# Overlapped Ghost blocks with a reloaded transposed x, look-up masks from ScalarE, and MLP weights through three raw buffers

## The reference

```
xn = layernorm(x)
h = rmsnorm(xn) -> q, k (8 heads x 32), v (8 x 64), output gate o, gates i and f (8 each)
Dmat[s,t] = F[s] - F[t] + i[t], causal;  m = rowmax(Dmat);  C = (q k^T / sqrt(32)) * exp(Dmat - m)
attn = C / max(|rowsum C|, exp(-m)) @ v;  rms norm per head, * sigmoid(o);  x1 = xn + attn @ w_out
attention block = x1 + (silu(rms(x1) @ w_gate) * (rms(x1) @ w_up)) @ w_down          # 512 -> 2048 -> 512
w = lut[idx]  (16 values; gate, up: 1376 x 512, down: 512 x 1376)
Ghost = (silu(xn @ w_g^T) * (xn @ w_u^T)) @ w_d^T                                     # 512 -> 1376 -> 512
```

## Time and profile before

| | before |
|---|---|
| median of three runs | 2892.45 us (2889.81 to 2893.76) |
| the profiled execution: its own time / its span | 2881.09 / 2879.3 us |
| TensorE busy (matmul) | 2558.6 us, 89% |
| VectorE busy | 1382.3 us, 48% |
| ScalarE busy | 837.6 us, 29% |
| GpSimd busy | 628.6 us, 22% |
| mean granted TensorE clock | 0.949 |
| moved | 508.94 MB, 177 GB/s |

### The profile page before, as it was taken

One profiled execution on the slowest core, in us unless ns is written; L12 is line 12 of the kernel. 1 busy time (PEld: TensorE's weight loads), 2 busy tenths in 40 slices (PEclk: granted clock), 3 DMA queues, 4 the chain that ended last, 5 costly groups with the idle time before them and its releaser, 6 DMA issues.

```text
span 2879.3 us, 33321 instructions
## 1 busy us (share of the span) xinstructions
PE 2558.6 (89%) x11152; PEld 2045.8 (71%) x11152; DVE 1382.3 (48%) x2444; ACT 837.6 (29%) x1522; POOL 628.6 (22%) x496
## 2 busy tenths in 40 slices
PE   6667999899899999889989988999889889889888
PEld 5345787687677777768767766777767767767767
DVE  4543645674675675567367466611323313323323
ACT  4323214434433442443443344211111111111111
POOL 2533221221221222132122122211111111111111
PEclk9578999999999999999999999999999999999999
DMA  4555442354255346136435424654654664664664
GB/s 147 209 201 215 147 168 92 132 192 158 96 182 218 103 154 241 63 124 217 155 120 187 177 106 154 234 201 167 249 212 160 245 223 165 245 221 165 248 217 164
DMA packets 121659, 508.94 MB, mean 177 GB/s; under 512 B 11376, under 2 KB 11376, under 8 KB 88080
## 3 DMA queue, kind: packets, MB, share of 16 engines
q1 hardware_dynamic: 115152, 494.89, 48.4%
q10 hardware_dynamic: 6336, 11.80, 1.2%
HBM read 434.69 MB, written 71.96 MB: 176 GB/s over the span
## 4 chain that ended last, share of the span: by engine, by line
PE 44%; issue 38%; POOL 7%; DVE 6%; DMA 2%; ACT 2%; DVEq 0%; POOLq 0%; SPq 0%; ACTq 0%
PE acc L561 10%; PE up_bank L561 9%; PE gate_bank L561 8%; PE bank_b L561 5%; PE bank_a L561 5%; POOL hidden_lo L1648 4%; PE bank_a L637 2%; PE bank_b L634 1%; PE bank_a L596 1%; DMA gu<-mlp_parts 1%; DVE look_w L1244 1%; PE bank_b L644 1%; PE bank_b L626 1%; DMA raw_dn<-w_dn 1%; POOL vw L1679 1%
## 5 line engine op out<-in xcount | busy, mean ns | idle before, releaser
L561 PE MATMUL gate_bank<-act_hi,gu 128*128 128x512 f32 x1728 | 605.4, 412 | 99.5 <-DMA gu<-ghost_parts 71.7
L1648 POOL TENSOR_TENSOR hidden_lo<-hm,hidden_hi 128x512 fp32r<-128x512 f32 x216 | 285.0, 1319 | 1480.2 <-ACT hidden_hi L860 1480.2
L561 PE MATMUL up_bank<-act_hi,gu 128*128 128x512 f32 x1728 | 593.9, 405 | 0.0
L561 PE MATMUL acc<-dn,hidden_hi 128*128 128x512 f32 x1728 | 559.7, 406 | 32.5 <-POOL hidden_lo L1648 32.5
L561 PEld LDWEIGHTS gate_bank<-act_hi,gu 128*128 128x128 f32 x1728 | 341.1, 197 | 184.5 <-issue 105.5
L1249 DVE SCALAR_TENSOR_TENSOR th<-th,gate_bank 128x512 f32<-128x512 f32 x216 | 147.6, 683 | 579.5 <-ACT th L855 579.5
L561 PEld LDWEIGHTS acc<-dn,hidden_hi 128*128 128x128 f32 x1728 | 326.6, 195 | 100.6 <-POOL hidden_lo L1648 20.3
L561 PEld LDWEIGHTS up_bank<-act_hi,gu 128*128 128x128 f32 x1728 | 326.7, 189 | 80.9 <-issue 13.5
L561 PE MATMUL gate_bank<-act_lo,gu 128*128 128x512 f32 x864 | 350.8, 406 | 0.0
L561 PE MATMUL acc<-dn,hidden_lo 128*128 128x512 f32 x864 | 344.2, 398 | 0.0
L561 PE MATMUL up_bank<-act_lo,gu 128*128 128x512 f32 x864 | 338.6, 392 | 0.0
(11 more groups left out here) (213 smaller groups left out, 3204.0 us busy)
## 6 DMA issues: line engine op xcount, KB each, us to landing
gu<-mlp_parts SPq DMA_DIRECT2D x128, 1024.0 KB, 5.2
gu<-ghost_parts SPq DMA_DIRECT2D x89, 1024.0 KB, 5.1
dn<-mlp_parts SPq DMA_DIRECT2D x128, 512.0 KB, 4.8
dn<-ghost_parts SPq DMA_DIRECT2D x88, 512.0 KB, 3.9
ghost_parts<-look_w SPq DMA_DIRECT2D x33, 512.0 KB, 3.0
mlp_parts<-gu SPq DMA_DIRECT2D x16, 1024.0 KB, 4.9
xn<-x SPq DMA_DIRECT2D x15, 1024.0 KB, 7.8
vo_w_hi<-vo_parts SPq DMA_DIRECT2D x12, 1024.0 KB, 9.7
```

Of the source, the lines that this page charges most:

```text
L561: mm = pe.matmul(dst, l[a], r[c], start=first and k == 0 and n == 0, stop=last and k == len(lhs) - 1 and n == 2)
L1648: pool.tensor_tensor(HH[1][:], hm[:], HH[0][:].bitcast(f32), ALU.subtract).then_inc(of.low.sem, 1)
```

## The change

**Ghost part.** Eight blocks written out one behind the other. The last `down` of a block (and that of the last MLP tile) comes behind the next block's `gate(0)` and `up(0)`. In the stage of every block SP stores its transposed x, high and low, to a new DRAM array (2 MB a block), and reloads it in tiles 1 and 2 of the Ghost block before; no layer norm and no transposes there. SP's row transfers stand one a tile in tiles 1 to 6. The sums are added by VectorE behind tile 0's `product` of the next block. The last block's output goes out in four pieces.

**Look-up.** ScalarE makes the masks of bits 1 to 3 as floats that are zero or not, from the index itself (Abs and Relu with constants), so a chunk has seven steps on VectorE beside bit 0 and 14 on ScalarE. Ten chunks for a pair of blocks (five and five), five more in `tiles(TAIL)`. A function `plan` writes out the steps of each tile under the caps ROOM_V and ROOM_A. In a unit's tile VectorE's steps and `norm_1` stand ahead of its `unit_3`. `upper` and `lower` of a chunk are called for in the same tile, SP stores it a tile later. One buffer holds the finished pair.

**MLP weights and the first block.** A tile's three parts are loaded, split and stored together (1536 columns). Tiles 0 to 11 go through two buffers that lie where the second block's transposed x comes later, 12 to 15 through a third. Four are split in `front(FIRST)`, eight beside the units, four in `front(SECOND)`. The second x is loaded into `raw_gu` in tile 1, its statistics taken in tiles 4 and 6. The first block's h2 steps move into `front(SECOND)`, with the ACC banks for the output projection. V and O weights are stored in tile 2 of the second block.

```diff
+PER_PAIR = 10
+CHUNKS = [(0, 5), (5, 10)]
+LEFT = 5
+STEPS_V = 7
+SELECTS = [(2, 3, 1), (5, 4, 1), (1, 0, 1), (6, 7, 1), (2, 1, 2), (5, 6, 2), (2, 5, 3)]
+STEPS_A = ["y", 3, "z", 2, "m1", 4, 5, "m3", 0, 1, 7, "m2", 6, "upper"]
+COUNTED = len(STEPS_A) - 1
+FREED_BY = {3: 4, "m1": 4, 4: 2, 0: 3, 1: 5, 7: 4, "m2": 6, 6: 6, "upper": 7}
+FREED_BY_OTHER = {5: 7, "m3": 7}
+NEEDED = ["m1", 5, 1, 6, 6, 6, 6]
+ROOM_V = [[0, 0] + [2] * 6 + [3, 3] + [4] * 5 + [0]] * 2 + [[3] * 15 + [0]]
+ROOM_A = [[5] * 8 + [7] * 7 + [0]] * 2 + [[7] * 15 + [0]]
...
+    first, end = span_of(kind)
+    n_a = len(STEPS_A)
+    v, a, uppers, rows = first * STEPS_V, first * n_a, first, []
+    for t in range(NM):
+        v_seen, up_seen = v, uppers
+        for _ in range(ROOM_A[kind][t]):
+            n, q = divmod(a, n_a)
+            what = STEPS_A[q]
             need = 0
...
+            if what in FREED_BY and n > first:
+                need = (n - 1) * STEPS_V + FREED_BY[what]
+            if what in FREED_BY_OTHER and n > first + 1:
+                need = (n - 2) * STEPS_V + FREED_BY_OTHER[what]
+            if a == end * n_a or need > v_seen or (what == "upper" and uppers > up_seen):
+                break
+            if what == 2 and n > first + 1 and up_seen < n - 1:
+                break
+            uppers += what == "upper" and n > first
+            a += 1
+        for _ in range(ROOM_V[kind][t]):
+            n, q = divmod(v, STEPS_V)
+            if v == end * STEPS_V or a < n * n_a + STEPS_A.index(NEEDED[q]) + 1:
+                break
+            v += 1
+        rows.append((v, a, uppers))
...
+        xt_parts = nc.dram_tensor("xt_parts", (BATCH * HALVES, 2, P, KT * TOK), f32, kind="Internal").ap()
+        with nc.sbuf_tensor("raw_mlp", [P, 2, 3 * D], f32) as raw_mlp:
+            pass
+        XH = [XH0, [sb(f"act1_{s}", [P, KT, TOK], f32r) for s in ("hi", "lo")]]
...
+            def load_mlp(m):
+                if m == NM - 4:
+                    wait(sp, vec_ln, FIRST, 0, f"xn{NB - 1}")
+                elif m > NM - 4:
+                    sp.wait_ge(mlp_lo, m)
+                elif m >= 2:
+                    sp.wait_ge(mlp_lo, m - 1)
+                sp.dma_start(raw_part(m), w_mlp[m]).then_inc(ld_mlp[raw_slot(m)], 16)
...
+            def load_xt(n, s):
+                dst = XH[n % 2][s][:, :, :].rearrange("p k n -> p (k n)").bitcast(f32)
+                sp.dma_start(dst, xt_parts[n, s]).then_inc(ld_xt[n % 2], 16)
...
+            blocks = [(BATCH + n // HALVES, n % HALVES) for n in range(BATCH * HALVES)]
+            for n, at in enumerate(blocks):
+                half = at[1]
+                for t in range(NF):
+                    if t + 1 < NF:
+                        load_gu(GHO, at, t + 1)
+                    elif n + 1 < len(blocks):
+                        load_gu(GHO, blocks[n + 1], 0)
+                    if n == 0 and t == NF - 1:
+                        sp.wait_ge(st_pad, 16)
+                    load_dn(GHO, at, t)
+                    if t in (1, 2) and n + 1 < len(blocks):
+                        if t == 1 and n:
+                            wait(sp, GHO.up, blocks[n - 1], NF - 1)
+                        elif t == 1:
+                            wait(sp, MLP.up, (BATCH, -1), NM - 1)
+                        load_xt(n + 1, t - 1)
+                    if t == 3:
+                        if n:
+                            wait(sp, vec_out, blocks[n - 1], NB - 1)
+                            sp.dma_start(rows_of(out, (n - 1) * TOK), rest[1 - half]).then_inc(st_out[1 - half], 16)
                         else:
...
+                            wait(sp, vec_out, (BATCH, -1), NB - 1)
+                            sp.dma_start(rows_of(mlp_rows, (BATCH * HALVES - 1) * TOK), XN[0][:]).then_inc(st_mlp[0], 16)
+                    if t == 4:
+                        sp.wait_ge(st_out[half], 16 * (n // 2 + 1))
+                        sp.dma_start(rest[half], rows_of(x, n * TOK)).then_inc(ld_rest[0], 16)
+                    if t == 5:
+                        sp.wait_ge(vec_rest.sem, vec_rest.before(at))
+                        sp.dma_start(rest[2], rows_of(x1_rows, n * TOK)).then_inc(ld_rest[1], 16)
+                    if t == 6:
+                        if n == 0:
+                            for z in range(2):
+                                sp.wait_ge(st_mlp[z], 16 * BATCH)
+                        sp.dma_start(rest[3], rows_of(mlp_rows, n * TOK)).then_inc(ld_rest[2], 16)
...
+            behind = (MLP, (BATCH, -1), NM - 1)
+            for n in range(BATCH * HALVES):
+                at = (BATCH + n // HALVES, n % HALVES)
+                for t in range(NF):
+                    gate(GHO, at, t, XH[at[1]])
+                    up(GHO, at, t, XH[at[1]])
+                    of, place, k = behind
+                    down(of, place, k, NM - 1 if of is MLP else NF - 1)
+                    behind = (GHO, at, t)
+            down(GHO, at, NF - 1, NF - 1)
...
+                if what == "y":
...
+                    ins = act.activation(yz[:, 0, :], ix[:, n % 2, :], ACT.Abs, bias=-7.5)
+                elif what == "z":
+                    act.wait_ge(look_act, in_act(at, n, "y"))
+                    ins = act.activation(yz[:, 1, :], yz[:, 0, :], ACT.Abs, bias=-4.0)
+                elif what == "m1":
+                    act.wait_ge(look_act, in_act(at, n, "z"))
+                    ins = act.activation(mask_of(n, 1), yz[:, 1, :], ACT.Relu, bias=-2.0)
+                elif what == "m2":
+                    ins = act.activation(mask_of(n, 2), yz[:, 0, :], ACT.Relu, bias=-4.0)
+                elif what == "m3":
+                    ins = act.activation(mask_of(n, 3), ix[:, n % 2, :], ACT.Relu, bias=-7.5)
+                else:
+                    if what == 3:
+                        act.wait_ge(look_b0, count(at, PER_PAIR, n + 1))
+                    if what == 2 and n >= first + 2:
+                        act.wait_ge(ghost_lo, count(at, PER_PAIR, n - 1))
+                    ins = act.activation(level_of(n, what), bit0(), ACT.Identity, bias=lt[:, 2 * what:2 * what + 1],
+                                         scale=ld[:, what:what + 1])
...
                         if t in (2, 4, 6):
                             norm_2(t // 2 - 1)
                         unit_2(t)
...
+                        if looks(at):
+                            look_up(at, steps_taken(half, t))
+                        if t % 2:
+                            norm_1(t // 2)
                         unit_3(t)
                         if t in (2, 4, 6):
...
+                if first:
+                    ln_apply(at, XN[1], 1, x_raw)
+                    for i in range(NB):
+                        x1_(at, i)
                     for i in range(NB):
                         x_T(at, i)
...
+                    for i in range(NB):
...
+                    if t == 0 and n == 0:
+                        wait(dve, MLP.down, (BATCH, -1), NM - 1)
+                        for i in range(NB):
+                            dve.tensor_copy(XN[0][:, i, :], ACC[i][:]).then_inc(vec_out.sem, 1)
+                    elif t == 0:
+                        add_ghosts(previous(at))
```

More of the change, by code:

```diff
@@ L60, with steps_taken, uppers_by @@
+PLANS = [plan(kind) for kind in range(3)]
+def steps_taken(kind, t):
+    return PLANS[kind][t][0]
+def uppers_by(kind, t):
+    return span_of(kind)[1] if t == NM - 1 else PLANS[kind][t][2]
 CAP = 15.0
@@ new lines, in program, with bit0, mask_of, in_act @@
+        pair = look_w[:, 4:6, :]
+        def level_of(n, k):
+            if k == 2:
+                return look_w[:, 6 + n % 2, :]
+            if k == 5:
+                return look_w[:, 8 if n % 2 else 15, :]
+            return look_w[:, {3: 0, 0: 1, 1: 2, 4: 3, 6: 9, 7: 10}[k], :]
+        def bit0():
+            return look_w[:, 11, :].bitcast(i32)
+        def mask_of(n, k):
+            if k == 3 and n % 2:
+                return raw_dn[:]
+            return look_w[:, 11 + k, :]
+        def in_act(at, n, what):
+            return count(at, PER_PAIR * COUNTED, n * COUNTED + STEPS_A.index(what) + 1)
@@ new lines, in tiles @@
+                    if looks(at) and t >= (UNITS if stage else 0):
+                        look_up(at, steps_taken(look_kind(at), t))
+                    if stage and not first:
+                        if t == 11:
+                            ln_stats(at, XN[1 - half], 1 - half, b * 16 + (16 + 16 * half))
+                        if t == 12:
+                            ln_square(at)
+                        if t == 13:
+                            ln_apply(at, XN[1 - half], 1 - half)
+                if first:
+                    ln_apply(at, XN[1], 1, x_raw)
+                    for i in range(NB):
+                        x1_(at, i)
@@ L1524, in tiles @@
                     for i in range(NB):
                         x_T(at, i)
-                if first:
+                    for i in range(NB):
+                        h2_(at, i)
```

(20 more changed lines are left out.)

770 lines of the change are left out of this document (372 added, 398 removed).

## The result

| | before | after |
|---|---|---|
| median | 2893.11 us (4 runs, 2889.81 to 2899.07) | 2614.46 us (4 runs, 2613.49 to 2617.44) |
| ratio | | 0.9037 [0.902, 0.9053] |
| profiled execution, its span | 2879.3 us | 2615.3 us |
| mean granted clock | 0.949 | 0.974 |

The change takes 278.6 us off by the medians and 264.0 by the spans. Most of the difference lies in the kernel before: its single runs reached from 2877 to 2905 us in later comparisons, and the profiled one was a short one. All that follows is reckoned on the spans, where the forecast was 252.5; the forecast of 2640 us lies 1% above the time, which is inside the range.

The account below looks back on a forecast made before the run. TensorE, busy nearly everywhere, was taken as the bound, losing time to waits and low clock. -146 - 96 - 11 + 0.5 = -252.5 from 2881.09 gives 2628.6; with 11.4 for the runs' median, 2640 us, range 2604 to 2695 (8 in 10).

Parts of the forecast that it names:

- Ghost part, -146: Ghost blocks: 88 tiles of 8.16 us in one row plus the end, 734.4 us against 880.4.
- If that cover went, it would cost 20: Ghost block edges: without gate and up covering the sums' adds before the next down, 7 x 2.9 = 20 us.
- The rival of late row transfers: Ghost part: at 280 GB/s heavy tiles run 1.2 us too long, 48 tiles cost some 75, total 2715; chance 0.08.
- Look-up, -96: Six blocks with a look-up: its cost of 137.0 us falls to 41, reckoned against the second block's 175.19.
- (b): Look-up cost that stays, per block: `norm_2(3)` stands behind its root on GpSimd, 0.9 us.
- (d): Look-up cost that stays, per block: seven ScalarE steps in tile 10 hold `hidden_hi`, 1.7 us, 3.2 with low clock.
- (c): Look-up cost that stays, per block: three selects in tile 9 stand before tile 10's h2 steps, 1.2 us.
- (a): Look-up cost that stays, per block: ScalarE starts late in three even tiles, `ct` ends after TensorE's `up`, 1.5 us.
- ScalarE as the bound: Rival, beside the units: 14 ordered steps push `exp` in every tile, +98 us, total 2738 at most; chance 0.11.
- First two blocks, -11: Start to second block's MLP: `front` plus four splits of 11.6 us, store and reload end at 246, against 257.42.
- `front` starts 20 us earlier: Second block's `front`, waiting only for four transposes with copies some 4 us behind the last `x1`: 20 us earlier.
- 0.5 us for the first mask: Start of the last MLP pass: the first mask waits on the index load, +0.5 us.

Follow-up runs that it names:

- light_plan: Kernel after with only the planner's caps ROOM_V and ROOM_A changed (three selects in tiles 2, 4, 6; no ScalarE look-up step in tile 10): 2707.26 us, ratio 0.937.

## Why the prediction was right, and where it was off

The mechanisms of the two large terms held. That the sum came so close is in part luck: by the stretches of the table the forecast missed by +16.2, -2.3, -4.2, -20.8, +2.7 and -3.2 us, 49 without the signs, and 11.5 with them. The 2640 us also carry 11.4 for the kernel before's short profiled execution, which has no counterpart in the kernel after. The 4.2 us of the fronts were not looked into.

- **Ghost part, -146 against -149.2: right in its steps.** The 88 tiles stand 8.16 us apart, one wait of 2.2 us is left, the adds lie under the next block's `gate` and `up`. "If that cover went, it would cost 20": 16.7 measured, though by `hidden_lo` and not by the adds. The 3.2 us of the miss are at the end: the last twelve matmuls ran at the spacing of the high clock (2.7 for 4.6) and the last 256 KB took 2.8 us for 4. The spread of the transfers over tiles 1 to 6, costed at nothing by bytes, is worth 77 us against one burst. The rival of late row transfers did not come true: TensorE never waits for `gud` here, and the mean of this part is 257 GB/s.
- **Look-up, -96 against -116.8.** The miss of 20.8 has two parts. I took the second block of the kernel before as the bound without a look-up (175.19), but the move of `norm_1` shortens that block too, to 172.92: 6 x 2.3 = 13.6. And the remainder came to 33.8 us, not 41. Of its terms (b), `norm_2(3)`, was too small (1.2 on average for 0.9). (d), the ScalarE steps that hold `hidden_hi` in tile 10, was too large: a wait of 1.0 for `hidden_lo` beyond the one that every block has, for 3.2. (c), the h2 steps, came to 0.6 for 1.2. In place of (a), a late `ct` in even tiles, stood a late `tt`, 1.3. The rest of the 5.6 is TensorE's busy time. I had counted that all VectorE work fits between `heads` and the next mask, but not that `tt` is wanted before the mask is.
- **ScalarE as the bound: no.** It is busy for 38.84 of 79.2 us beside the units. What a unit's tile can't bear is a VectorE step that waits for a ScalarE step of the same tile, as light_plan showed; that the plan had none beside the units was the right thing to look for.
- **First two blocks, -11 against +5.2: the step that failed.** "`front` starts 20 us earlier" became 10, and the chain was mis-sized. From unit 7 of the first block to `front` the 20 us did come (36.1 for 55.9), but I had taken all that lies ahead as unchanged. `front` lost 4.8 us in the first block's units, by the longer norm and its new place, and 5.0 ahead of them, of which single runs account for up to 2.7 (unit 0 stood at 67.6 to 70.3 us over the kernels here); where the rest of the 5.0 comes from stays open. Then three distances of 11.6 became 13.7 on average, since I took the load at 5.9 us from a 512 KB row for one of 768 KB, which landed 7.5 to 8.5 after its issue: 6 us. The reload landed in 6.8 and not in 5. I had named "the first block's units slow down because GpSimd splits weights" as a sign of error, and gave it no price.
- **Last pass, +0.5 against +3.2.** "0.5 us for the first mask" overlooked what is queued behind it: the mask waits 12 us for an index load, and `gated` with it.

## What to carry to other kernels

Ask of each wait not only whether it is hidden, but what is queued behind the waiting instruction on its engine: several of the costs here (`gated` behind a mask, `act_lo` behind a select, a store behind a reload, `tt` behind a norm) were of that kind. When work moves to an idle engine, see which operations of its neighbours it lengthens, and keep those off the chain that TensorE waits for. A chain of equal steps through one buffer costs load plus work for each step: a second buffer, even one pieced together from idle ones, was worth more than the shorter way to its start.

## What was not expected of the hardware

- A VectorE operation on 8 columns with two SBUF inputs took 1002 ns on average, up to 1970, beside GpSimd's subtracts of 512 columns, and 172 ns without them. The reciprocal, with a single input, kept 203 ns, but another step with one input took 0.85 us beside such a subtract, for 0.17.
- An SP issue of a 1 MB transfer, 0.4 us as a rule, took 5.29 us as the last of six in a row, and 1.40 as the fourth.
- A wait of 2.6 us cost a stretch 4.4 (TensorE's busy time +1.8, granted clock 0.98), while seven waits of 2.2 us in the Ghost part cost 16.7 us together, hardly more than themselves.
- The queues held 394 GB/s over 17.5 us in which reads dominate. By the Trainium skill (DMA: Bandwidth & Descriptors, Specifications) the HBM limit is about 358 a core; as in the earlier trace rows, the measurement stands above it.
